# Two chunks of an adaLN block closed through TensorE: residual and bias enter the PSUM banks as products with the identity, and the last norm reads the banks

## The reference, cut to what matters

```python
h = _layernorm(x) * (1 + ca) + sa
x = x + ga * _L1_attn_ref(h, ...)          # state-space scan, then y @ W_out.T
h = _layernorm(x) * (1 + cb) + sb
x = x + gb * _L1_ffn_ref(h, ...)           # fft, product with w_freq, inverse fft, + bias
# _L1_attn_ref, the scan over time, for 256 channels and 16 states:
h = exp(dt_t * A) * h + dt_t * xv_t * B_t
y_t = einsum('bdn,bn->bd', h, C_t)
y = y * silu(z); return y @ W_out.T
# _L1_ffn_ref is linear: one 128 x 128 matrix (w_fft in the kernel) and a bias row
```

## Time and profile before

| | |
|---|---|
| three runs | 566.05 us median (565.32 to 568.63) |
| the profiled execution | 565.65 us, span 563.5 us |
| VectorE busy | 430.1 us, 76% |
| TensorE matmul busy | 466.0 us, 83% |
| ScalarE, GpSimd busy | 342.8 us, 348.1 us |
| mean granted TensorE clock | 0.956 |

### The profile page before, as it was taken

How to read it: one execution, slowest core, us unless ns; L and a number is a source line. 1 busy time by engine, 2 the same in 40 slices (tenths; PEclk the granted TensorE clock), 3 DMA queues, 4 the chain that set the end, 5 groups by cost and what they waited for, 6 DMA issues and landing times.

```text
span 563.5 us, 6814 instructions
## 1 busy us (share of the span) xinstructions
PE 466.0 (83%) x2324; PEld 327.2 (58%) x2324; DVE 430.1 (76%) x706; ACT 342.8 (61%) x461; POOL 348.1 (62%) x250
## 2 busy tenths in 40 slices
PE   4879898689899999988889988879979757397566
PEld 4457566345788887766766666756767532042224
DVE  5789998963542541169897799998799998989994
ACT  1445253433655564699998999988999738453310
POOL 3137997946404123316496669798668898789561
PEclk9998897999999999999999999999999959787998
DMA  8800000000000000402846853668554568731100
GB/s 274 332 1 0 1 1 2 0 0 0 1 1 2 0 2 1 151 1 73 189 112 135 204 149 83 145 140 177 152 151 112 135 149 172 199 81 69 56 0 19
DMA packets 15601, 48.93 MB, mean 87 GB/s; under 512 B 2320, under 2 KB 7824, under 8 KB 12624
## 3 DMA queue, kind: packets, MB, share of 16 engines
q0 software_dynamic: 3024, 22.02, 19.5%
q1 hardware_dynamic: 11968, 25.58, 13.3%
q10 hardware_dynamic: 576, 0.92, 0.5%
HBM read 25.31 MB, written 1.18 MB: 47 GB/s over the span
## 4 chain that ended last, share of the span: by engine, by line
PE 33%; DVE 30%; ACT 12%; POOL 10%; issue 9%; DMA 4%; POOLq 0%; SPq 0%; DVEq 0%; ACTq 0%
PE pO L1368 9%; DVE Hs L824 7%; DVE S L709 6%; DVE pCT L811 5%; POOL ZS L394 4%; PE pY L1423 4%; DVE pH L708 3%; DMA Acc<-ZS 3%; PE pH L1356 3%; ACT gel L1072 3%; ACT dA L1084 3%; ACT L1084 2%; PE pH L1358 2%; PE pH L1357 2%; POOL ln_x L359 2%
## 5 line engine op out<-in xcount | busy, mean ns | idle before, releaser
L1368 PEld LDWEIGHTS pO<-w_e,gel 128*128 128x128 f32 x1024 | 122.2, 192 | 13.9 <-issue 8.7
L1368 PE MATMUL pO<-w_e,gel 128*128 128x128 f32 x1024 | 124.7, 276 | 1.3 <-DVE X L795 1.0
L824 DVE TENSOR_TENSOR_SCAN Hs<-dA,HL,pCT 128x512 f32<-128x512 f32 x96 | 117.7, 1267 | 6.3 <-POOL ZS L394 3.2
L1072 ACT ACTIVATE gel<-pH,b_e 128x512 f32<-128x512 f32 x128 | 86.1, 687 | 40.1 <-PE pH L1358 39.3
L1084 ACT ACTIVATE dA<-dt,a_neg 128x512 f32<-128x512 f32 x128 | 81.9, 711 | 21.8 <-DVE Hs L824 21.5
L394 POOL TENSOR_TENSOR ZS<-Hs,Crow 128x1024 f32<-128x1024 f32 x31 | 74.9, 2428 | 30.3 <-DVE Hs L824 28.8
L811 DVE TENSOR_TENSOR pCT<-u,pB 128x1024 f32<-128x1024 f32 x64 | 78.3, 1224 | 10.0 <-PE pB L1448 8.9
L1356 PE MATMUL pH<-h2h,w_e1h 128*128 128x512 f32 x128 | 57.5, 449 | 21.4 <-ACT gel L1072 20.3
L795 DVE SCALAR_TENSOR_TENSOR X<-pO,wts,X 128x128 f32<-128x128 f32 x128 | 36.0, 344 | 44.2 <-PE pO L1368 43.5
L394 POOL TENSOR_TENSOR Zev<-Hs,Crow 128x1024 f32<-128x1024 f32 x26 | 62.7, 2426 | 8.3 <-DVE Hs L824 7.7
L1448 PE MATMUL pB<-ST,sel 96*128 96x512 bf16 x64 | 26.6, 415 | 38.8 <-DVE pCT L811 38.6
(11 more groups left out here) (251 smaller groups left out, 851.7 us busy)
## 6 DMA issues: line engine op xcount, KB each, us to landing
Crow<-c_rows SPq DMA_DIRECT2D x32, 512.0 KB, 4.2
Acc<-ZS POOLq DMA_DIRECT2D x12, 1024.0 KB, 8.8
Acc<-Zev POOLq DMA_DIRECT2D x9, 1024.0 KB, 7.4
w_e<-in_w_e SPq DMA_DIRECT2D x2, 2048.0 KB, 10.6
X<-in_x SPq DMA_DIRECT2D x4, 256.0 KB, 7.7
S<-in_w_mod ACTq DMA_DIRECT2D x2, 384.0 KB, 5.6
out<-h2T SPq DMA_DIRECT2D x3, 256.0 KB, 2.8
w_cx<-in_conv_row SPq DMA_DIRECT2D x1, 512.0 KB, 8.8
```

What stands on the lines that cost most here:

```text
L824: vec.tensor_tensor_scan(Hs[:, 2 * o + d, 0:w], dA[:, 4 * (p % 2) + 2 * o + d, 0:w], pU[:, d, 0:w], HL[:, d, n:n + 1] if c else 0.0, ALU.m ...
L1072: nc.scalar.activation(gel[:, n % NG, 0:w], pH[n % 2][:, 0:w], ACT.Gelu_apprx_tanh, bias=b_e1[:, NK * e + k:NK * e + k + 1]).then_inc(s["m ...
L1368: ins = mm(pO[:, j * P:(j + 1) * P], gel[:, n % NG, j * P:(j + 1) * P], w_e2[:, NK * (g % E) + k, :], start=(k == 0 and j == 0), stop=(k = ...
```

## The change

From the third chunk on (`APART = 2`), `project` starts its bank with X through a product with the identity (one 128x512) and adds the products with w_out to it; ScalarE copies the bank to X, and VectorE only waits for that. `fft` starts its bank with the bias row and X through two products with the identity; ScalarE copies the bank to outb. GpSimd's `bias` and VectorE's two additions are gone for c = 2. For the fourth chunk, `project_last` writes two banks, pH0 and pH1, 256 columns each, that begin with X through two 128x256 products with the identity and signal one by one (`cl_o`); `tail_x` is gone, and `close` takes statistics and the normalised rows from the banks, and copies them to X by two 128x256 copies ahead of the last addition.

```diff
@@ later_stages, closing of the fourth chunk
-            for stage in (("A", "total", NL * NP - 1), ("end", "gate", last), ("A", "project", last), ("end", "tail_x", last),
+            for stage in (("A", "total", NL * NP - 1), ("end", "gate", last), ("A", "project", last),
@@ gpsimd, bias(c)
+                if c >= APART:
+                    return
@@ vector, close()
+                Xp = [PS[h][:, 0:2 * P].rearrange("p (j d) -> p j d", d=P) for h in range(2)]
                 for h in range(2):
+                    vec.wait_ge(s["cl_o"], h + 1)
                     for j in (2 * h, 2 * h + 1):
-                        ins = vec.bn_stats(ln_st[:, j, :], Xc[:, j, :])
+                        ins = vec.bn_stats(ln_st[:, j, :], Xp[h][:, j % 2, :])
...
-                        ins = vec.tensor_scalar(ln_x[:, j, :], Xc[:, j, :], ln_mv[:, j, 0:1], ln_rs[:, j:j + 1],
+                        ins = vec.tensor_scalar(ln_x[:, j, :], Xp[h][:, j % 2, :], ln_mv[:, j, 0:1], ln_rs[:, j:j + 1],
                                                 ALU.subtract, ALU.mult)
                     ins.then_inc(s["cl_xn"], 1)
+                for h in range(2):
+                    ins = vec.tensor_copy(Xc[:, 2 * h:2 * h + 2, :], Xp[h])
+                link(ins)
@@ vector, tail_x(c) and fft(c, b)
+                if c >= APART:
+                    vec.wait_ge(s["mam_x"], c + 1)
+                    return
...
+                if c >= APART:
+                    return
@@ scalar, new; both return at once for c < APART
+            def tail_x(c, b):
+                act.wait_ge(s["mam_o"], c + 1)
+                nc.scalar.copy(rows_of(X, c), tokens(PS[b], c)).then_inc(s["mam_x"], 1)
+            def fft(c, b):
+                act.wait_ge(s["fft_o"], c + 1)
+                act.wait_ge(s["out_done"], 16 * c)
+                act.wait_ge(s["h2_lo"], NL)
+                nc.scalar.copy(outb[:, 0:blocks(c), :], tokens(PS[b], c)).then_inc(s["fft_x"], 1)
@@ tensor, project_last(c)
+                pe.wait_ge(s["moe_acc"], NL * E)
+                for h in range(2):
+                    if h in held:
+                        pe.wait_ge(s[held[h][0]], held[h][1])
+                    mm(PS[h][:, 0:2 * P], ident[:, :], rows_of(X, c)[:, 2 * h:2 * h + 2, :], start=True, stop=False,
+                       skip_group_check=True)
                 for d in range(ND):
                     pe.wait_ge(s["mam_y2"], 2 * c + d + 1)
                     for j in range(NJ):
+                        h = j // 2
+                        ins = mm(PS[h][:, j % 2 * P:(j % 2 + 1) * P], y2[:, d, j * P:(j + 1) * P], w_out[:, d, :],
+                                 start=False, stop=(d == 1 and j % 2 == 1), skip_group_check=True)
+                        if d and j % 2:
+                            ins.then_inc(s["cl_o"], 1)
@@ tensor, project(c, b), behind the wait for mam_y2
+                if c >= APART:
+                    pe.wait_ge(s["moe_acc"], E * (c + 1))
+                    mm(PS[b][:, :], ident[:, :], rows_of(X, c), start=True, stop=False, skip_group_check=True)
@@ tensor, fft(c, b)
                 pe.wait_ge(s["ln_evac"], E2[c])
+                if c >= APART:
+                    pe.wait_ge(s["mam_x"], c + 1)
+                    mm(PS[b][:, :], ident[:, 0:1].to_broadcast([P, P]), bias_row[:, None, :].to_broadcast([P, NJ, P]),
+                       start=True, stop=False, skip_group_check=True)
+                    mm(PS[b][:, :], ident[:, :], rows_of(X, c), start=False, stop=False, skip_group_check=True)
```

More of the change, by code:

```diff
@@ L39 @@
 NL = len(WIDTHS)
+APART = 2
 ALONE = (NL * E - AHEAD) // 2 * 2
@@ L242, in build @@
             mam_st mam_cd mam_bB mam_ub mam_dA mam_sc mam_z mam_zs  mam_y mam_y2 mam_o mam_x
-            mam_zl0 mam_zl1 mam_yl cl_st cl_rs cl_xn cl_tr cl_ev cl_mm cl_x fft_o fft_b fft_x vec_chain act_chain pool_chain out_done""".split()
+            mam_zl0 mam_zl1 mam_yl cl_o cl_st cl_rs cl_xn cl_tr cl_ev cl_mm cl_x fft_o fft_b fft_x vec_chain act_chain pool_chain out_done""".split()
         s = {n: sem(n) for n in names}
@@ L1085, in decays @@
                                          scale=a_neg[:, r % 2, n:n + 1]).then_inc(s["mam_dA"], 1)
+            def tail_x(c, b):
+                if c < APART:
+                    return
+                act.wait_ge(s["mam_o"], c + 1)
+                nc.scalar.copy(rows_of(X, c), tokens(PS[b], c)).then_inc(s["mam_x"], 1)
+            def fft(c, b):
+                if c < APART:
+                    return
+                act.wait_ge(s["fft_o"], c + 1)
+                act.wait_ge(s["out_done"], 16 * c)
+                act.wait_ge(s["h2_lo"], NL)
+                nc.scalar.copy(outb[:, 0:blocks(c), :], tokens(PS[b], c)).then_inc(s["fft_x"], 1)
             def turned(c, which, b):
@@ L1102, in run @@
                         continue
[L1103 to L1106, removed]
+                    if stage in ("ln_turn", "route", "turn", "x_part", "rows", "dt_part", "z_part", "project", "fft"):
+                        {"project": tail_x, "fft": fft, "ln_turn": turned, "route": route, "turn": turn, "x_part": x_part, "rows": rows, "dt_part": dt_part,
                          "z_part": z_part}[stage](c, *k, stage_bank(p, at))
             for p, stages in later_stages():
+                if p == NL * NP:
+                    close()
+                    break
                 if 0 <= p + AHEAD < NL * E:
@@ L1482, in totals_of, with project_last @@
                 total(p, 1)
-            def project_last(c, b):
-                use(b, "mam_x", c + 1)
+            def project_last(c):
+                pe.wait_ge(s["moe_acc"], NL * E)
[4 more added lines that the diff above has]
+                       skip_group_check=True)
                 for d in range(ND):
@@ L1488, in project_last @@
                     for j in range(NJ):
-                        ins = mm(PS[b][:, j * P:(j + 1) * P], y2[:, d, j * P:(j + 1) * P], w_out[:, d, :],
-                                 start=(d == 0 and j == 0), stop=(d == 1 and j == NJ - 1), skip_group_check=True)
-                ins.then_inc(s["mam_o"], 1)
+                        h = j // 2
[3 more added lines that the diff above has]
+                            ins.then_inc(s["cl_o"], 1)
             def close():
@@ L1512, in project @@
                 if c == NL - 1:
-                    return project_last(c, b)
+                    return project_last(c)
                 pe.wait_ge(s["mam_y2"], 2 * c + 2)
@@ L1520, in project @@
                         ins = mm(PS[b][:, j * P:(j + 1) * P], y2[:, d, j * P:(j + 1) * P], w_out[:, d, :],
-                                 start=(d == 0), stop=(d == 1))
+                                 start=(d == 0 and c < APART), stop=(d == 1 and (c < APART or j == NJ - 1)),
+                                 skip_group_check=(c >= APART))
                 ins.then_inc(s["mam_o"], 1)
@@ L1526, in fft @@
                 pe.wait_ge(s["ln_evac"], E2[c])
+                if c >= APART:
[3 more added lines that the diff above has]
+                    mm(PS[b][:, :], ident[:, :], rows_of(X, c), start=False, stop=False, skip_group_check=True)
                 for j in range(blocks(c)):
-                    ins = mm(PS[b][:, j * P:(j + 1) * P], h4T[:, j * P:(j + 1) * P], w_fft[:, :], start=True, stop=True)
+                    ins = mm(PS[b][:, j * P:(j + 1) * P], h4T[:, j * P:(j + 1) * P], w_fft[:, :], start=(c < APART),
+                             stop=(c < APART or j == NJ - 1), skip_group_check=(c >= APART))
                 ins.then_inc(s["fft_o"], 1)
```

## The result

The changed kernel takes 564.3 us (median of 20 runs, 562.30 to 568.12) against 567.0 us of the kernel before (20 runs of its own, 564.58 to 569.41); the ratio is 0.9956 with a 95% interval of 0.994 to 0.9971. That is 0.44% or 2.5 us faster (the two medians differ by 2.7); by the interval 0.3 to 0.6%, 1.6 to 3.4 us. Two executions of this study, 680 us in e1 and 774 us in e5, had a mean granted clock of 0.65 and 0.56 and are left out of the ratios. The forecast was 2.55 us of 565.65, a ratio of 0.9955; its absolute figure, 563.2, is 1.1 too low, mostly since the kernel before had a median of 566.05 in the three runs shown and of 567.0 in all twenty.

What follows compares the result with a forecast made beforehand. VectorE was taken to bound the kernel until state 63, then a chain hopping between engines. Savings of 0.72 + 1.43 + 0.4 = 2.55 us from 565.65 give 563.1; forecast 563.2 us, range 561.9 to 565.9.

Steps and rivals of the forecast that it cites:

- Pair 26: Third chunk's project, after state 53: VectorE loses the addition to X and its gap, 0.72 us saved.
- The hand-over to ScalarE: After state 53: ScalarE's copy has X ready by 507.2, 1.3 us before VectorE asks at 508.48.
- the unmoved decays: Pair 28's decays, queued behind ScalarE's copy, wait for state 53 and start at 508.51: not delayed.
- GpSimd's 0.6 us: GpSimd's output of state 54 keeps 0.6 us to spare before the scans of state 56, so the saving holds.
- Pair 28: Third chunk's fft, after state 57: VectorE loses a 0.71 us wait, a 0.69 addition and a gap, 1.43 us saved.
- The cover over the two products: TensorE's row of state 59: 1.5 us to spare, less one short product, before VectorE wants it.
- The close: Fourth chunk's end: statistics start 0.5 us earlier, less 0.11 for normalising from PSUM, 0.4 us saved.
- the costs of PSUM: Reading banks in the close: 0 for statistics, 54 ns for each of two normalisings on the path, 0.11 us together.
- rival (d): The close gains nothing because banks are slow to read, 0.1 us more per operation: 563.6 us; chance 0.10.
- Rival (a): The close runs at full clock because TensorE's idle time shrinks: 562.3 us; chance 0.25.
- the first reading: While the fourth chunk's states run, work in VectorE's queue between two states lengthens the kernel one for one.

Runs made afterwards that it cites:

- e1: Kernel before with only the third chunk's project changed; state 53 to 54 took 1.24 us against 1.96, ratio 0.996 to 1.0006.
- e5: Changed kernel with the close's two products with X ahead of the last total; ratio 0.9949 (0.9929 to 0.9969), profile at granted clock 0.56.
- e2: Kernel before with only the third chunk's fft changed; state 57 to 58 took 0.03 us against 1.43, ratio 0.9962 to 1.0004.
- e7: Changed kernel with three more 128x512 products ahead of the third chunk's fft; state 58 to 63 took 23.86 us against 22.46, ratio 0.9961 to 1.0001.
- e3: Kernel before with only the fourth chunk's close changed; statistics 0.49 us earlier, ratio 0.9987 to 1.0021.
- e4: Changed kernel with VectorE instead of ScalarE emptying the third chunk's two banks; ratio 1.0006 to 1.0039 against the kernel before.
- e8: Changed kernel with the second chunk closed the same way (APART = 1); ratio 0.9924 to 0.9966, state 53 to end 51.75 us.
- e9: Changed kernel without the close's one filling 128x512 product; statistics to last addition 6.52 us, 0.50 longer, ratio 0.9941 to 0.9982.
- e10: Same kernel as e5, run again for a profile; time to statistics 4.16 us against 4.83 in the changed kernel, ratio 0.9923 (0.9896 to 0.9949).
- e11: The e10 kernel with two filling products in the close instead of one; state 53 to end 51.14 us, ratio 0.9932 (0.9909 to 0.9956).
- e6: Kernel before with three filling products in the close instead of one; statistics to last addition 5.92 us against 6.68, ratio 0.9961 to 1.0008.

## Why the prediction was right

- **Pair 26: 0.72 forecast, 0.72 measured** (changed, e1). The hand-over to ScalarE with 1.3 us of slack, the unmoved decays and GpSimd's 0.6 us all held.
- **Pair 28: 1.43 forecast, 1.40 measured** (changed 1.39, e2). The cover over the two products was put at 1.5 us less a short product; it is 1.29 in the profile and 1.2 by e7's loss.
- **The close: 0.4 forecast, 0.40 measured at equal clock.** The statistics gained 0.49 (0.5). Of the costs of PSUM, statistics cost next to nothing (0.50 against 0.49 for two) and a normalising 64 ns (407 against 343; 54 taken), 0.13 for the second pair, which is on the path, in place of 0.11. Of this 0.03 comes back, since that pair starts 2.97 us behind the statistics' start and not 3.00. So rival (d), which needed 0.1 us more for each operation, is out. By the Trainium skill, page "VectorE: DVE Perf Modes", section "The TRN2 errata", an operation that reads PSUM has a fixed part longer by 65 ns; in the statistics this does not show, and the trace disagrees with it there. By the same page, section "Why PSUM operands drop a tier", an f32 operation with one input loses in PSUM the double rate that it has in SBUF, as an estimate 67 ns for 128 elements; the 64 ns of the normalising agree with that.
- **Rival (a), not the forecast's case, is what the profile of the changed kernel shows** in the close: 3.24 us gained from state 53 to the end, 0.7 more than the forecast. It was given 0.25. The ratio does not decide between the two: its interval, 1.6 to 3.4 us, holds 2.55 and 3.24 alike, so that it came out at 2.5 is in part luck. Eight profiles have the new close: with its filling product (changed, e3, e4, e7, e8) the clock stayed in all five, without it (e9) it fell; with the products moved ahead it fell once (e10) and with more filling it didn't (e11). The old close lost it in two of three (before and e2, not e1) and kept it with more filling (e6). By these counts a higher chance would have been right. What decides the clock there stays open.
- **What was off** is the absolute figure. The prediction's own sum is 563.1 and 0.4 for the median, which makes 563.5 and not the 563.2 that it states. The rest is the base, a median of three runs of a kernel whose runs spread over 5 us: the measured medians of the kernel before went from 565.06 to 567.0 in this study, and the range should have reached higher for it.

The 22.46 us from state 58 to the end of state 63 in every kernel but e7 bear out the first reading, that VectorE bounds there. The sum over the stages in the profiles is 0.72 + 1.39 + 0.49 + 0.66 = 3.26, of 3.24 between 55.02 and 51.78; 0.72 + 1.39 + 0.40 = 2.51 of it is the change at equal clock. The ratio's interval has room for both sums.

## What to carry to other kernels

An addition after a matmul is worth moving into the accumulation only if a second engine with idle time then empties the bank: with VectorE itself emptying it (e4), the kernel became slower: by the time of the added products in pair 28, where VectorE waits for the bank, with nothing gained in pair 26. Check the emptying engine's place in its own queue, as the second chunk shows, where the copy stood behind 3.8 us of other work and came 1.6 us after the bank was ready. Put the products that bring X into the bank ahead of TensorE's last wait, not behind it (e10); and when runs spread by more than the effect, measure between two landmarks inside the profile.

## What the runs showed of the hardware

In single profiles the granted clock at the end of the kernel went with work that has no other use. Without one 128x512 product (0.86 us of TensorE time) the clock fell in the close and cost 0.50 us (e9), while in five profiles of the new close with that product it held; with more of such products it held in both kernels tried (e6, e11). It is no rule: e1 kept the clock with 1.74 us of idle time ahead of the transposes, e10 lost it with 0.78.

The clock in 32 to 72 us, while TensorE was busy for some 34 of the 40 us, differed between executions of the same instructions (0.91 or 0.85 to 0.86), and went with an attention whose last scan started up to 3.4 us later. What decides it was not tested.

A normalising of 128x128 took 407 ns from a PSUM bank and 343 from SBUF, while the statistics of 128x128 took 290 and 285: what reading a bank costs differs from one operation to the next.
